# Recurrence of a gated delta layer: four of the eight transition columns summed on TensorE, and the transitions' spread moved between the halves of the query sums

## The reference, cut to what matters

```python
def step(S, inp):
    q_t, k_t, v_t, g_t, b_t = inp
    S = S * jnp.exp(g_t)[..., None, None]
    mem = jnp.einsum('bhk,bhkv->bhv', k_t, S)
    delta = (v_t - mem) * b_t[..., None]
    S = S + jnp.einsum('bhk,bhv->bhkv', k_t, delta)
    o_t = jnp.einsum('bhk,bhkv->bhv', q_t, S)
    return (S, o_t)
S0 = jnp.zeros((q.shape[0], H, DK, DV), q.dtype)
_, o = jax.lax.scan(step, S0, (qt, kt, vt, gt, bt))
```

## Time and profile before

| | us |
|---|---|
| median of three runs (lowest, highest) | 812.0 (808.83, 813.77) |
| the profiled execution | 814.66 |
| its span | 812.9 |
| busy in the span: PE, DVE, ACT, POOL | 754.6, 535.0, 268.1, 218.5 |
| mean granted clock of TensorE | 0.977 of full speed |

### The profile page before, as it was taken

The page is one execution under the profiler, slowest core; times in us unless marked ns, Lnnn a source line. Parts: engine busy times, 40 slices in busy tenths (PEclk is TensorE's granted clock), DMA queues, the critical chain, the costliest instruction groups (busy, mean ns, idle before and its releaser), DMA issues. The chain is left out here.

```text
span 812.9 us, 11547 instructions
## 1 busy us (share of the span) xinstructions
PE 754.6 (93%) x4010; PEld 555.8 (68%) x4019; DVE 535.0 (66%) x1323; ACT 268.1 (33%) x424; POOL 218.5 (27%) x188
## 2 busy tenths in 40 slices
PE   5988999999999999999999499999987999999995
PEld 4422332467788888887545388777863999999995
DVE  4797997268555555554799989999677453343345
ACT  2465677544334343433573212021341100000000
POOL 4542000022223232321012000577102344444321
PEclk9999999989999999999999899999998999999997
DMA  8595000100111111131031503400005999999972
GB/s 299 153 208 107 2 3 2 44 35 20 45 53 42 55 41 56 40 114 61 3 115 52 220 0 100 134 1 1 1 28 184 349 347 337 341 352 343 338 260 86
DMA packets 39333, 101.04 MB, mean 124 GB/s; under 512 B 5374, under 2 KB 19894, under 8 KB 38326
## 3 DMA queue, kind: packets, MB, share of 16 engines
q1 hardware_dynamic: 35334, 91.06, 34.7%
q0 software_dynamic: 3504, 8.98, 2.9%
q10 hardware_dynamic: 448, 0.39, 0.2%
HBM read 84.17 MB, written 16.44 MB: 124 GB/s over the span
## 5 line engine op out<-in xcount | busy, mean ns | idle before, releaser
L1381 PE MATMUL psum<-xr,wr 128*128 128x512 f32 x600 | 146.8, 396 | 1.0 <-DVE arena L2043 1.0
L1381 PEld LDWEIGHTS psum<-xr,wr 128*128 128x128 f32 x600 | 114.6, 191 | 25.6 <-issue 1.7
L735 POOL TENSOR_TENSOR wr<-ring,wr 128x512 fp32r<-128x512 f32 (+1 forms) x50 | 55.0, 1118 | 240.0 <-ACT wr L918 147.5
L1703 PEld LDWEIGHTS psum<-arena 128*128 128x128 f32 x700 | 83.5, 192 | 3.2 <-issue 1.5
L1703 PE MATMUL psum<-arena 128*128 128x128 f32 x700 | 84.0, 276 | 1.1 <-ACT arena L1134 1.1
L1713 PE MATMUL psum<-arena 128*128 128x256 f32 x350 | 81.4, 380 | 0.0
L2509 DVE TENSOR_SCALAR arena<-psum,arena 128x256 f32<-128x256 f32 x35 | 16.9, 484 | 93.8 <-PE psum L1713 93.8
L1891 DVE TENSOR_REDUCE small<-psum 128x1 f32<-128x512 f32 x112 | 71.1, 685 | 9.9 <-PE psum L1257 9.2
L1392 PE MATMUL psum<-hr,wr 128*128 128x512 f32 x300 | 76.6, 392 | 0.9 <-DVE hr L1980 0.9
L2006 DVE TENSOR_TENSOR hid<-hid,psum 128x512 f32<-128x512 f32 x50 | 34.4, 688 | 60.2 <-ACT hid L924 60.0
L893 ACT ACTIVATE arena<-psum 128x1024 f32<-128x1024 f32 x64 | 63.1, 1023 | 29.3 <-PE psum L1267 28.5
(11 more groups left out here) (392 smaller groups left out, 1214.3 us busy)
## 6 DMA issues: line engine op xcount, KB each, us to landing
arena<-in_w1u SPq DMA_DIRECT2D x35, 642.5 KB, 5.9
arena<-in_w1d SPq DMA_DIRECT2D x35, 640.0 KB, 5.4
ring<-in_w SPq DMA_DIRECT2D x25, 384.0 KB, 3.0
z_scratch<-w_a SPq DMA_DIRECT2D x4, 768.0 KB, 7.2
arena<-z_scratch SPq DMA_DIRECT2D x8, 384.0 KB, 6.5
arena<-part_scratch SPq DMA_DIRECT2D x9, 256.0 KB, 7.4
qkv_scratch<-arena SPq DMA_DIRECT2D x4, 512.0 KB, 2.6
arena<-qkv_scratch SPq DMA_DIRECT2D x4, 512.0 KB, 4.0
```

What stands on the lines that cost most here:

```text
L735: pool.tensor_tensor(wr0[:, k, LO, part], ring0[:, k, part], wr0[:, k, HI, part], ALU.subtract).then_inc(s["w0_lo"], 1)
L1381: ins = pe.matmul(bank[2 * b + m][:, :], wr0[:, k, w, lo:lo + P], xr[:, x, f, half(b)], start=(f == 0 and (w, x) == PARTS[0]), stop=(f == ...
L1703: ins = pe.matmul(bank[2 + r % 2 * 3 + k // 2][:, tile(k % 2)], wup1[:, r % NW, lo:lo + P], xgT[:, r % 2, f, :], start=(f == 0), stop=(f = ...
```

## The change

Columns 4 to 7 of the transitions are no longer summed by VectorE. It forms their four products in one go into buffers of their own (the space of offset products that are already summed; two waits on `n_sum` guard that), and TensorE adds them with 32 matmuls over 128 columns into banks 2 and 6, between the offset sums and the query sums. ScalarE copies them into `Msb` in two copies ahead of the copies of the query sums. VectorE does columns 2 and 3 as before and then waits for these copies before it touches the diagonal. On TensorE the query sums are cut in two: t=0 to 3, then `spread_m(0)` and `spread_m(1)`, then t=4 to 7. The other edits shift the thresholds of semaphores by the added counts.

```diff
--- before.py
+++ after.py
@@ -269,6 +269,9 @@
         mprod = [arena[:, 3 * DV * CT + n * DK * CT:3 * DV * CT + (n + 1) * DK * CT]
                  .rearrange("p (j x c) -> p j x c", j=C, x=DK) for n in range(2)]
         assert 3 * DV * CT + 2 * DK * CT <= end
+        M_PE, M_BANKS = range(4, DK), (2, 6)
+        mterms = [arena[:, at0:at0 + DK * CT].rearrange("p (j x c) -> p j x c", j=C, x=DK)
+                  for at0 in (2 * DV * CT, 2 * DV * CT + DK * CT, 0, DK * CT)]
         Nsb = arena[:, end:end + DV * CT]
         Msb = v2[:, 0:CC * DK * DK]
         Nscan = arena[:, end + 4 * CT * DK + 2 * CT:][:, 0:DV * CT]
@@ -756,13 +759,13 @@
                     ch.link(ins)
             ins.then_inc(s["decays"], 1)
 
-            pool.wait_ge(s["x_prod"], 2 * C + O_OWN)
+            pool.wait_ge(s["x_prod"], 2 * C + len(M_PE) + O_OWN)
             pool.wait_ge(s["scan_lo"], 1)
             for t in range(O_OWN, C):
                 if t == C - 1:
-                    pool.wait_ge(s["n_sum"], DK + 3)
+                    pool.wait_ge(s["n_sum"], DK + 5)
                 o_product(pool, t).then_inc(s["x_prod"], 1)
-            pool.wait_ge(s["x_prod"], 3 * C)
+            pool.wait_ge(s["x_prod"], 3 * C + len(M_PE))
 
             pool.wait_ge(s["qB_first"], 16 * VG * 2)
             for u, (n0, count) in enumerate(UNITS[:SUMMED + 1]):
@@ -1052,6 +1055,11 @@
                                n_bank(k).rearrange("p (g v c) -> p g v c", g=VG, v=VV), ACT.Copy).then_inc(s["n_in"], 1)
             for x in range(2):
                 act.wait_ge(s["n_sum"], DK + x + 1)
+                act.activation(Msb.rearrange("p (c k x) -> p k x c", c=CC, k=DK)[:, M_PE[0] + 2 * x:M_PE[0] + 2 * x + 2],
+                               bank[M_BANKS[x]][:, 0:2 * CT].rearrange("p (k x c) -> p k x c", k=2, x=DK),
+                               ACT.Copy).then_inc(s["n_in"], 1)
+            for x in range(2):
+                act.wait_ge(s["n_sum"], DK + 2 + x + 1)
                 act.activation(Qp.rearrange("p (x c t) -> p t x c", x=DK, c=CC)[:, 4 * x:4 * x + 4],
                                bank[x].rearrange("p (t x c) -> p t x c", t=4, x=DK), ACT.Copy)\
                    .then_inc(s["qp_in"], 1)
@@ -1523,7 +1531,7 @@
             pe.wait_ge(s["ld_sel"], 64)
 
             def o_sum(t):
-                pe.wait_ge(s["x_prod"], 2 * C + t + 1)
+                pe.wait_ge(s["x_prod"], 2 * C + len(M_PE) + t + 1)
                 for j in range(t + 1):
                     ins = pe.matmul(bank[t // 2][:, t % 2 * 256:(t % 2 + 1) * 256], ident[:, :],
                                     o_prod(t)[:, j].rearrange("p x c -> p (x c)"),
@@ -1537,7 +1545,16 @@
                                     start=(j == 0), stop=(j == C - 1), skip_group_check=True)
                 ins.then_inc(s["n_sum"], 1)
 
-            for t in range(C):
+            for n, k in enumerate(M_PE):
+                pe.wait_ge(s["x_prod"], 2 * C + n + 1)
+                for j in range(C):
+                    ins = pe.matmul(bank[M_BANKS[n // 2]][:, n % 2 * CT:(n % 2 + 1) * CT], ident[:, :],
+                                    mterms[n][:, j].rearrange("p x c -> p (x c)"),
+                                    start=(j == 0), stop=(j == C - 1), skip_group_check=True)
+                if n % 2:
+                    ins.then_inc(s["n_sum"], 1)
+
+            def queries(t):
                 pe.wait_ge(s["x_prod"], DK + t + 1)
                 to = bank[t // 4][:, t % 4 * CT:(t % 4 + 1) * CT]
                 pe.matmul(to, ident[:, :], qa[:, t * CT:(t + 1) * CT], start=True, stop=False, skip_group_check=True)
@@ -1558,8 +1575,12 @@
                 pe.matmul(bank[6 + h % 2][:, :], selg[:, h // 2, :], Msb[:, h % 2 * 512:(h % 2 + 1) * 512],
                           start=True, stop=True).then_inc(s["m_spread"], 1)
 
+            for t in range(C // 2):
+                queries(t)
             spread_m(0)
             spread_m(1)
+            for t in range(C // 2, C):
+                queries(t)
             pe.wait_ge(s["qp_in"], 2)
             for t in range(O_OWN):
                 ins = o_sum(t)
@@ -2292,14 +2313,19 @@
                                   ALU.mult).then_inc(s["x_prod"], 1)
             ch.need(quartered)
             state["ended"][1] = last_sum(1)
-            for k in range(2, DK):
+            for n, k in enumerate(M_PE):
+                if n % 2 == 0:
+                    dve.wait_ge(s["n_sum"], DK - 2 + n // 2)
+                product(mterms[n], k, DV, XR).then_inc(s["x_prod"], 1)
+            for k in range(2, M_PE[0]):
                 products(k)
                 if k > 2:
                     ch.need(quartered)
                     state["ended"][(k - 1) % 2] = last_sum(k - 1)
                 quartered = tree(k)
             ch.need(quartered)
-            ch.need(last_sum(DK - 1))
+            ch.need(last_sum(M_PE[0] - 1))
+            dve.wait_ge(s["n_in"], DK + 2)
             diag = Msb.rearrange("p (c e) -> p c e", c=CC)[:, :, 0:DK * DK:DK + 1]
             dve.tensor_tensor(diag, diag, by_step(A0)[:, C - 1, :].unsqueeze(2)
                               .broadcast_to((P, CC, DK)), ALU.add).then_inc(s["m_done"], 1)
```

## The result

The changed kernel takes 816.57 us in the median of 21 runs; the kernel before, 812.23 us over the same number. The ratio is 1.0046, 95% interval 1.003 to 1.0063: 3.7 us slower, between 2.4 and 5.1. It is estimated without one run of the kernel before that took 2702.03 us, and it is not the quotient of the two medians (1.0053). The profiled execution of the changed kernel took 819.73 us, its span is 816.7 us (before 814.66 and 812.9).

The account below looks back on a forecast made before the run. VectorE was taken as late before the scan, with TensorE hardly earlier and nearly full, and the scan as setting all that follows. Delays of 1.1 + 0.3 + 1.5 = 2.9 us on 812.0 gave 814.9 us, own range 812.5 to 817.5.

Parts of the forecast that it names:

- DVE early: On VectorE before the scan: diagonal at 504.6, output products ending at 511.0 instead of 515.83, a gain of 4.9 us.
- Added sums: On TensorE between offset and query sums: 32 matmuls, 64 records at 0.113 us each, 7.2 us in all.
- First reduction: At the scan's start: held by the slot fill behind ACT's second query copy, 517.3 instead of 516.23, +1.1 us.
- Steps 16 and 24: In the scan: DVE waits for TensorE's third and fourth spreads, 0.3 and 1.5 us.
- POOL and the transfers: Output and state products and the query write and reads: later, but covered by 3 us, so no added cost.
- Rival A: TensorE between 503.9 and 517.1 doesn't hold back DVE's gain: -4.9 us, 807.1 us; chance 6%.
- Rival B: On TensorE, the added records run faster than the query sums', 2.0 us less: +0.9, 812.9 us; chance 7%.
- C: From 533 on, state products, query transfers or spreads for steps 40 and 56 come late: +5.5, 817.5 us; chance 13%.
- D: On TensorE, added records cost 0.233 us as at 256 columns, 7.7 more: +10.6, 822.6 us; chance 4%.
- a shift of the scan is a shift of the kernel, one for one: Behind the scan: all that follows waits for its end, so its +2.9 us passes unchanged into the kernel's time.
- scan term: The scan's whole delay: +1.1 at the first reduction, +0.3 at step 16, +1.5 at step 24, +2.9 us.
- left the clock out: TensorE's granted clock was 1.00, full level, over the query sums beside the added work, so no term was given.

Follow-up runs that it names:

- early slot: The changed kernel with the first slot filled on ACT ahead of the second query copy, step 4 waiting for the second slot; ratio 1.0052 to the kernel before.
- early spreads: The changed kernel with the third spread after output sum 4, the fourth ahead of the first state sum, later spreads and state copies moved; ratio 1.0032 to the kernel before.
- scan first: The changed kernel with both first slots ahead of the second query copy, and spreads and state copies placed for an early scan; ratio 1.0034 to the kernel before.
- order alone: The kernel before with only a new order of the later spreads and state copies, all columns still on VectorE; ratio 1.0041.
- shift alone: The kernel before with two of six output products formed twice by VectorE, putting the scan off without more TensorE work; ratio 1.0062.
- more filler: The changed kernel with 40 instead of 30 filler matmuls ahead of the second layer's routing sums; ratio 1.005 to the kernel before.

## Why the prediction came out as it did

The forecast was 814.9 us, 2.9 above before; measured are 816.57, 4.3 above the median of the same set and 3.7 by the ratio. The interval of the ratio, 2.4 to 5.1, holds the 2.9.

The mechanism is the one of the text, wait by wait. DVE early: diagonal forecast at 504.6, found at 504.95; new wait on ACT's copy forecast at 0.2, found 0.35. Added sums forecast at 7.2 us, found 7.1. First reduction held by the slot behind the query copy: forecast 517.3, found 517.12. Counted from the end of the offset sums its shift is 0.68 and not 1.1: 0.2 of that is the later start of this profile, and the slot starts 0.2 before the copy ahead of it ends, and the reduction follows the first slot. Steps 16 and 24: forecast 0.3 and 1.5, found 0.31 and 1.16; TensorE's work from the third spread's end to the fourth's, put at 8.0 us, took 7.8. POOL and the transfers stayed covered, and the later spreads made no wait. Sum in the trace 2.30 instead of 2.9.

The runs took the parts away one at a time. The early slot showed that the 5.38 us of wait, the largest in the profile, is not the cost; the early spreads took 1.6 of the 2.3 away. Rival A, that DVE's gain goes through, fell on the reason given against it, TensorE's 3.3 us of idle for 7.2 us of sums: even with the whole scan 4.2 us earlier nothing was won. Rival B, cheap sums, fell with 0.112 us a record. The Trainium skill (TensorE: Matmul & The Clock Gate, section Back-to-back issue gap) has about 81 ns for a pair of weight load and matmul at 128 columns; for float32 records this trace disagrees again. C, a second round of stalls, didn't occur, nor D, dear sums. D's 0.233 a record was too high even for 256 columns at the full clock, since the 29.88 us behind it hold the first offset sums at half the clock; the 56 records of the output sums took 0.216 each before (511.79 to 523.88).

Where the forecast was short is the step "a shift of the scan is a shift of the kernel, one for one". The scan's 2.3 us came with another 1.4 in the timed runs, and in the run that only shifted the scan 3.0 came with 2.0; both rests are just clear of zero by their intervals (0.1 to 2.8 and 0.2 to 3.8). That the near agreement of 2.9 with 3.7 rests on a scan term that was 0.6 too large and a rest that was not in the sum at all is luck, and has to be said. The prediction also left the clock out, because it was 1.00 beside the added work. It was there, in the changed kernel too. But over the whole execution the mean granted clock is lower by some 0.003 than that of the kernel before, which by the estimate above goes with 1.6 us. What lowers it, and what the rest of a kernel like scan first consists of, stays open; the profiles don't show it, since two executions of the kernel before differ behind the scan by 4.9 us.

## What to carry to other kernels

Before work is moved from a late engine to one that waits for it, count the receiver's idle up to the point where both are needed again: here the 3.3 us up to the diagonal could take two columns (3.6 us) and not four (7.2), and all idle up to the last gather, 7.6 us, was just enough for four to come out even in the best order. A copy or a spread that is moved ahead of other work delays everything behind it in that engine's text, which cost more here (1.4 us) than the added sums (0.9). The longest wait in a list may be free, if the next releaser comes at the same time regardless: only moving it shows. And one profile of each side is too little for a change of 0.5%, where two profiles of one kernel differ by more than that in stretches that the change doesn't touch.

## What the runs showed of the hardware that was not expected

TensorE, idle for 9.97 us in the middle of float32 sums, came back at a granted clock of 0.50 and stayed there for about 5.5 us, and a spread group took 3.78 us instead of 1.99. In two of the thirteen other profiles the clock fell between the offset sums and the last reduction too: behind a wait of 4.15 us with the order alone (0.57 from 517 to 521 us), and with the shift alone behind the same wait of 3.30 us for the diagonal after which the kernel before ran at 1.00 (0.67 from 504 to 508 us). Ten more filler matmuls ahead of a stretch with gaps of 1.0 to 1.6 us didn't hold the clock, and where it fell differed between profiles whatever the filler: 49.3 us behind the last reduction in the changed kernel, 54.9 with the slot early (old filler) and 54.5 with more filler. Eleven runs of the kernel with the shifted scan spread over 811.6 to 821.2 us; in the 21 of the changed kernel the fastest, 811.99 us, had a mean clock of 0.979 and the slowest, 822.58 us, one of 0.971.
